# Cross attention with transposed scores, row maxima subtracted on TensorE, and division after the values

## What is computed

```python
q = _rope(_heads(xq @ wq)); k = _rope(_heads(k)); v = _heads(v)     # 16 heads of 64
sim = jnp.einsum('bhnd,bhmd->bhnm', q, k) * DH ** (-0.5)            # n = 1024, m = 77
a = jax.nn.softmax(sim, axis=-1)
o = jnp.einsum('bhnm,bhmd->bhnd', a, v)
return o.transpose(0, 2, 1, 3).reshape(B, N, MID) @ wo + bo          # + x
```

## Time and profile before

| | us |
|---|---|
| median of 3 runs (2480.9 to 2484.71) | 2481.2 |
| the profiled execution, its own time | 2478.87 |
| its span, first to last instruction | 2477.1 |
| cross attention, first to last instruction of its own | 1719.9 to 2241.8 |
| PE busy in the span | 2228.5 (90%) |
| DVE busy | 1860.5 (75%) |
| ACT busy | 1330.3 (54%) |
| POOL busy | 355.7 (14%) |

### The profile page before, as it was taken

The page is one execution under the profiler, slowest core; times in us unless marked ns, Lnnn a source line. Parts: engine busy times, 40 slices in busy tenths (PEclk is TensorE's granted clock), DMA queues, the critical chain, the costliest instruction groups (busy, mean ns, idle before and its releaser), DMA issues. The chain is left out here.

```text
span 2477.1 us, 40034 instructions
## 1 busy us (share of the span) xinstructions
PE 2228.5 (90%) x15036; PEld 1042.1 (42%) x15036; DVE 1860.5 (75%) x2924; ACT 1330.3 (54%) x1655; POOL 355.7 (14%) x201
## 2 busy tenths in 40 slices
PE   2499999999999999999999999944899999994899
PEld 2133333344333344333334333442465656563566
DVE  6579989877989886899986998574766666666453
ACT  5266666755676654666664666443443443444221
POOL 3100000000000000000000000023554545452000
PEclk9699999999999999999999999967898999986899
DMA  5101010101111011101010110052322222224211
GB/s 163 54 35 36 35 44 35 39 32 44 52 40 40 27 44 44 52 27 44 35 44 35 52 36 27 19 160 72 94 85 85 85 85 85 85 85 128 67 38 34
DMA packets 106254, 143.81 MB, mean 58 GB/s; under 512 B 28209, under 2 KB 74367, under 8 KB 106111
## 3 DMA queue, kind: packets, MB, share of 16 engines
q1 hardware_dynamic: 106111, 141.87, 17.9%
HBM read 55.70 MB, written 12.85 MB: 28 GB/s over the span
## 5 line engine op out<-in xcount | busy, mean ns | idle before, releaser
L642 PE MATMUL sa_ps_o<-sa_probs,sa_v_pair 128*64 128x512 f32 x2048 | 532.7, 614 | 2.9 <-DVE sa_mx L897 2.9
L806 ACT ACTIVATE sa_probs<-sa_ps_s 128x1024 f32<-128x1024 f32 x512 | 495.8, 1025 | 27.9 <-PE sa_ps_s L629 27.9
L897 DVE CUSTOM_DVE_ANT_0 sa_rise<-sa_ps_t,sa_rise 128x512 f32<-128x512 f32 x504 | 327.9, 688 | 190.7 <-PE sa_ps_t L606 190.3
L910 DVE TENSOR_TENSOR sa_acc<-sa_acc,sa_probs 128x1024 f32<-128x1024 f32 x384 | 462.6, 1246 | 7.2 <-ACT sa_probs L806 7.2
L794 ACT ACTIVATE sa_rise<-sa_ps_t 128x1024 f32<-128x1024 f32 x252 | 257.7, 1023 | 250.0 <-PE sa_ps_t L599 250.0
L642 PEld LDWEIGHTS sa_ps_o<-sa_probs,sa_v_pair 128*64 128x64 f32 x2048 | 101.9, 134 | 246.4 <-issue 173.7
L576 POOL TENSOR_TENSOR sa_xr<-sa_xr,sa_bo_row 128x1024 f32<-128x1024 f32 x8 | 21.6, 2726 | 1280.1 <-DMA sa_xr<-in_x 1280.1
L622 PE MATMUL sa_ps_s<-sa_hi 64*128 64x512 f16 x1024 | 194.5, 376 | 0.0
L622 PE MATMUL sa_ps_s<-sa_hi,sa_lo 64*128 64x512 f16 x1024 | 194.4, 376 | 0.0
L622 PE MATMUL sa_ps_s<-sa_lo,sa_hi 64*128 64x512 f16 x1024 | 194.4, 376 | 0.0
L629 PE MATMUL sa_ps_s<-sa_m_line,sa_m_ones 64*128 64x512 f16 x1024 | 189.5, 377 | 3.7 <-DMA sa_m_line<-sa_m_rows 3.7
(11 more groups left out here) (275 smaller groups left out, 4613.5 us busy)
## 6 DMA issues: line engine op xcount, KB each, us to landing
sa_swp<-sa_raw SPq DMA_DIRECT2D x128, 256.0 KB, 2.4
ca_swp<-ca_raw SPq DMA_DIRECT2D x70, 256.0 KB, 2.4
sa_inv<-sa_scratch SPq DMA_DIRECT2D x128, 128.0 KB, 2.9
ca_q_hl<-ca_hi SPq DMA_DIRECT2D x68, 128.0 KB, 2.3
ca_q_hl<-ca_lo SPq DMA_DIRECT2D x68, 128.0 KB, 2.3
sap_xs<-in_x SPq DMA_DIRECT2D x4, 1024.0 KB, 7.1
sa_xr<-in_x SPq DMA_DIRECT2D x4, 1024.0 KB, 5.9
cap_xs<-x_after_self SPq DMA_DIRECT2D x4, 1024.0 KB, 7.2
```

The lines of the kernel that those rows point to most:

```text
L642: ins = pe.matmul(ps_o[rows(x), half(c)], v_pair[:, kt, rows(x)], probs[:, kt % 2, c, half(x)], start=(kt == 0), stop=(kt == NK - 1))
L806: act.activation(probs[:, kt % 2, c, :], ps_s[c][:, :], ACT.Exp, scale=float(DH) ** -0.5).then_inc(s_p, 1)
L897: dve.tensor_tensor_reduce(out=larger, in0=max_banks(j, t)[:, half(x)], in1=larger, scale=1.0, scalar=-3.0e38, op0=ALU.add, op1=ALU.max, a ...
L910: dve.tensor_tensor(acc[:, c, :], before, probs[:, kt % 2, c, :], ALU.add).then_inc(s_acc[c], 1)
```

## The change

`project_context` leaves the keys where they are made, in `k_hi` and `k_lo` (128 partitions, a pair of heads each), and its stacking DMAs are gone. `cross_attention` is new. Its loops are unrolled over g = 0 to 31. For each pair, by engine, in program order:

```diff
 TensorE
+            for g in range(G):
+                bases(g)                    # queries on partitions, hi x hi only, 16 products of 77 columns
+                project(g + 3, 0)           # waits: s_sum_r (sums of g - 2 evacuated)
+                pe.transpose(turn[1][0:2 * TT, 0:P], mx[:, g % 2, :], ident[:, :]).then_inc(s_mt, 1)
+                scores(g)                   # keys on 77 partitions, 12 products of 512 columns
+                values(g - 1)
+                pe.wait_ge(s_line, 16 * (g + 1))
+                shift(g)                    # 4 products: minus the row of maxima
+                totals(g - 1)               # 4 products of ones with the probabilities
+                project(g + 3, 1)
+                if output_batch(g) is not None: ...   # g = 10, 18, 26: the 8 output tiles
 ScalarE
+                evacuate_q(g + 3, 0)
+                row(g)                      # 16 x 128, waits for the transpose
+                high_output(g - 3)
+                exponentials(g, 0); exponentials(g, 1)
+                evacuate_o(g - 1, 0); evacuate_o(g - 1, 1)   # waits: s_pv, s_ot >= g - 2
+                evacuate_sums(g - 1)
+                evacuate_q(g + 3, 1)
+                high(g + 2)
 VectorE
+                maxima(g)                   # one reduce_max over 16 x 77 elements of PSUM
+                divide(g - 3)
+                turned(g + 2)               # two multiplications with the tables, one addition
+                low_output(g - 3)
+                reciprocals(g - 2)
+                low(g + 2)                  # waits: s_hi of g + 2
+                if output_batch(g) is not None: ...   # 8 residuals
 SyncE
+                gather_sums(g - 2)
+                swap(g + 2)
+                line(g)
+                spread_inverses(g - 2)
+                if output_batch(g) is not None:
+                    sp.wait_ge(s_yr, TT * (b + 1))
+                    sp.dma_start(y_v[b], xr[:]).then_inc(s_out, 16)
+                    sp.wait_ge(s_out, 16 * (b + 1))
+                    sp.dma_start(xr[:], x_v[b + 1]).then_inc(s_x, 16)
```

```diff
+        ps_s = ps("ps_s", [P, 2, N])
+        ps_o = ps("ps_o", [P, N])
+        ps_t = ps("ps_t", [P, N])
+            def line(j):
+                sp.wait_ge(s_mt_r, j + 1)
+                sp.dma_start(m_line[0:P:DH, :], m_rows[:]).then_inc(s_line, 16)
+            def gather_sums(g):
+                sp.wait_ge(s_sum_r, g + 1)
+                sp.dma_start(few[:], sums[0:P:32, :]).then_inc(s_few, 16)
+            def spread_inverses(g):
+                sp.wait_ge(s_rec, g + 1)
+                sp.dma_start(scratch.rearrange("n (i k) -> (n i) k", k=16), few[:]).then_inc(s_scr, 16)
+                sp.wait_ge(s_scr, 16 * (g + 1))
+                for x in range(2):
+                    sp.dma_start(inv[rows(x), :], scratch[2 * x:2 * x + 2].rearrange("a k -> (a k)")
+                                 .partition_broadcast(DH)).then_inc(s_inv, 16)
+            def bases(g):
+                for t in range(TT):
+                    at = t // 4 * HALF + t % 4 * M
+                    for x in range(2):
+                        ins = pe.matmul(ps_s[:, x, at:at + M],
+                                        hi[rows(x), g % 3, t * P:(t + 1) * P], k_hi[rows(x), pair, b, :],
+                                        start=True, stop=True)
+            def scores(g):
+                for c in range(2):
+                    for n, (k, q) in enumerate(((k_hi, hi), (k_lo, hi), (k_hi, lo))):
+                        for x in range(2):
+                            pe.matmul(ps_s[0:M, c, half(x)], k[rows(x), pair, b, :], q[rows(x), s, half(c)],
+                                      start=(n == 0), stop=False)
+            def maxima(g):
+                dve.wait_ge(s_base, g + 1)
+                banks = ps_s.rearrange("p c (x n) -> p (c x) n", x=2)[:, :, 0:4 * M]
+                dve.reduce_max(mx[:, g % 2, :], banks.rearrange("p a (t m) -> p a t m", m=M), AX_X).then_inc(s_max, 1)
+            def exponentials(g, c):
+                act.wait_ge(s_st, 2 * g + c + 1)
+                act.activation(probs[:, g % 2, c, :], ps_s[0:M, c, :], ACT.Exp, ...)
```

More of the change, by code:

```diff
@@ L1043, in _ @@
             for n in range(2):
[L1044 to L1051, removed]
+                sp.wait_ge(s_swap[n], 32)
         @block.tensor
@@ L1273, in transposes @@
-            def transposes(par, x):
-                for t in range(TT):
-                    ins = pe.transpose(ps_pt[0:M, t * P:(t + 1) * P], e[:, par, x, t, :], ident[:, :])
-                ins.then_inc(s_pt_w, 1)
+                b, pair = j // PAIRS, j % PAIRS
+                cols = slice(pair * P, (pair + 1) * P)
+                split_product(pe, turn[c], range(KD), wq, xT, lambda k: (slice(None), k, cols),
+                              lambda k: (slice(None), b, k, half(c))).then_inc(s_q, 1)
@@ new lines, in shift, with values @@
+            def shift(g):
+                for c in range(2):
+                    for x in range(2):
+                        ins = pe.matmul(ps_s[0:M, c, half(x)], m_ones[rows(x), 0:M], m_line[rows(x), half(c)],
+                                        start=False, stop=True)
+                    ins.then_inc(s_st, 1)
+            def values(g):
+                b, pair = g // PAIRS, g % PAIRS
+                for c in range(2):
+                    pe.wait_ge(s_p, 2 * g + c + 1)
+                    if g >= 1:
+                        pe.wait_ge(s_oev, 2 * (g - 1) + c + 1)
+                    for x in range(2):
+                        at = pair * P + DH * x
+                        ins = pe.matmul(ps_o[rows(x), half(c)], v_all[:, b, at:at + DH], probs[:, g % 2, c, half(x)],
+                                        start=True, stop=True)
+                    ins.then_inc(s_pv, 1)
@@ L1322, in _ @@
[L1322 to L1330 removed]
+            pe.wait_ge(s_init, 3)
@@ new lines, in _ @@
+            values(G - 1)
+            pe.wait_ge(s_sum_r, G - 1)
+            totals(G - 1)
+            most = KM - 3
+            pe.wait_ge(s_ot, G - 3)
+            for t in (0, 1, 2, 3, 5, 4, 6, 7):
+                if t == 0:
+                    pe.wait_ge(s_p, 2 * G)
+                if t == 5:
+                    pe.wait_ge(s_mt_r, G)
+                if t == 4:
+                    pe.wait_ge(s_sum_r, G)
+                if t == 6:
+                    pe.wait_ge(s_oev, 2 * G)
+                output(B - 1, t, range(most), True, False)
@@ L1458, in feed_forward @@
+            for g in range(G - 3, G):
+                divide(g)
+                low_output(g)
+                if g < G - 1:
+                    reciprocals(g + 1)
+            dve.wait_ge(s_xb, 2 * B)
+            for t in range(TT):
+                residual(B - 1, t)
 def feed_forward(nc, tag, x_src, x_dst, b1, b2, xT, w1, w2):
```

490 lines of the change are left out of this document (233 added, 257 removed).

## The result

The changed kernel takes 2517.1 us (median of 4 runs, 2515.7 to 2521.7) against 2481.1 for the kernel before (2477.7 to 2484.7 in the same comparison): a ratio of 1.0148, with a 95% interval of 1.0129 to 1.0167. The forecast was 2500 with a range of 2450 to 2525: the time lies inside the range, but the change is 36 us where 19 were forecast. The profiled execution has a span of 2515.2 us, 38.1 more than before; the next stage starts at 2281.1 instead of 2241.8, which is 39.3 later, so that all of it comes from the changed stages.

A forecast was written before the change was run, and what follows sets the result against it. Bound: a closed chain from VectorE's maxima through TensorE and ScalarE back, 11.6 us, plus clock falls. First maxima 1731.8 + intervals 483.9 + tail 45 = 2260.7 against 2241.8, 19 later: 2500 by the median, range 2450 to 2525.

The forecast's parts named there:

- The closed chain: Cross attention: VectorE's maxima through transpose, scores, values, shift, exponentials, evacuations, high, low to the next maxima; 11.6 us at full clock.
- A second chain is as long, SyncE's round hides.: Cross attention: low_output releases the values' evacuation, leading back to low_output, 11.8 us less overlaps; SyncE's inverses, sums, swap about 11.2, hidden.
- A sign that the prediction had put under "wrong": VectorE's divide waiting for the inverses in cross attention would count against the forecast; no size given.
- The clock: TensorE idle 2.8 us before each transpose: one clock fall per iteration, 1.75 us taken, ends 0 and 3.5; period 13.3.
- a period of 12.4 to 12.8: In-between rival: falls in half of the iterations, or several links two tenths shorter; 2478 to 2490; chance 0.18.
- The bases: TensorE's 16 products of 64 rows: at most 0.9 us by the skill page, 2.2 without it; outside the chain.
- The iteration behind the output projection: Iterations 11, 19, 27: SyncE waits 4.4 us for the store before the maxima row; 17.4, or 20.8 if queued; 19.3 taken.
- Head: Cross attention's start to the first row maxima: swap, turned, high and two lows, 18.2 us.
- Last interval and tail: Last interval 9.5 us, without high or low; then inverse round trips, last matmuls, residual and store, 45, ends 38 and 50.
- Warm: Rival: the clock does not fall in cross attention; period 11.6, 2454; chance 0.21.
- cold: Rival: idle time and a thinner queue keep the lower clock through scores and values; period 15.1, 2547; chance 0.07.
- The order is not the bound: Rival: engine work, not program order, sets the period; TensorE 9.4, VectorE 9.0; period 9.5, about 2400; chance 0.04.

The follow-up runs named there:

- the first experiment: Changed kernel with VectorE's low(g+1) moved behind maxima(g), instead of low(g+2) at the iteration's end: 2505.0 us, ratio 1.0105 to the kernel before.
- both edits together: Changed kernel with low(g+1) behind maxima(g) and reciprocals(g-2) right behind divide(g-3) on VectorE: 2450.4 us, ratio 0.9881 to the kernel before.
- the filled gap: Changed kernel with 11 unread products in TensorE's idle time ahead of each maxima transpose, except behind an output projection: 2496.9 us, ratio 1.0070.
- the queue moved: Changed kernel with y's store, the wait for its landing and the next x's load on GpSimd's queue instead of SyncE's: 2484.7 us, ratio 1.0019.
- the narrow bias: Changed kernel with GpSimd adding the output bias to 8 columns of x only, the rest left out: 2504.8 us, ratio 1.0094.
- the order mended and the queue moved: Changed kernel with low(g+1) behind maxima(g), reciprocals(g-2) behind divide(g-3), and y's store and x's load on GpSimd's queue: 2427.5 us, ratio 0.9791.

## Why the prediction was near, and where it was off

The time lay in the range, and the mechanism of the ordinary iterations was right. The closeness is in part luck: the stage ends 39 us later than before, not 19, and the largest term, 23 ordinary intervals, came out because the forecast had halved a span of 0 to 3.5 us for the clock. Forecast and measured, by the prediction's own terms, for the profiled execution:

| term | forecast | measured | difference |
|---|---|---|---|
| start of the stage | 1713.6 | 1715.9 | +2.3 |
| from there to the first M | 18.2 | 20.4 | +2.2 |
| interval 0 | 11.9 | 9.9 | -2.0 |
| 23 ordinary intervals | 305.9 | 304.7 | -1.2 |
| 3 with an output projection | 98.7 | 97.9 | -0.8 |
| 3 behind one | 57.9 | 73.3 | +15.4 |
| last interval | 9.5 | 11.7 | +2.2 |
| tail | 45 | 47.3 | +2.3 |
| next stage starts | 2260.7 | 2281.1 | +20.4 |

- **The closed chain.** Right. The trace has full-clock intervals of 11.5 against a sum of 11.6; the first three intervals are 8.1 to 9.6 once low has left the chain; and cutting it at a second place has about the same effect. Its links: maxima 1.434 against 1.43 worked out from the earlier trace rows; values 1.94 with 1.86 until the shift, 1.87 taken from the earlier trace rows.
- **"A second chain is as long, SyncE's round hides."** The second loop is what limited the first experiment, but not the one through s_ot that the prediction had, whose way to M over the evacuations, high and low is cut by the same move: it runs through the reciprocals and the inverses' transfers, as the gain of both edits together shows. The swap lands in 3.2 us (median), not the 2.4 of the earlier trace rows, and the inverses in 3.9, so that "about 11.2" was low. It did not matter for the forecast while the first chain was longer, but a fix of the first chain alone, priced by it, was priced too high (the first experiment's expectation). A sign that the prediction had put under "wrong" was there too: the divide waits for the inverses in 8 of the 23 ordinary intervals, for 0.5 to 1.3 us. VectorE waits for high behind it in any case.
- **The clock.** One fall per iteration at 1.7 was a good mean of a wrong picture. There are 21 falls in 31 intervals, and an ordinary interval has no slow stretch (8 of 23), a short one (8, 1.4 us longer) or one of 10.2 us (7, 4.0 longer). The forecast took the middle of its ends 0 and 3.5, and the mean came out at 1.75 over 11.5: the number was right by luck. The upper end was too low, since a slow stretch of 10.2 us also covers totals and projection, and these hold back the evacuations. That the falls cost time is shown by the filled gap (-20.2 us), though the fill's own cost hides how much in all. (Among the rivals, a period of 12.4 to 12.8 at 2.6 us per 0.1 us gives 2477 to 2487, not 2478 to 2490; nothing hangs on it.)
- **The bases.** The 16 products take 0.46 us (the row at 1792.62 above), less than the 0.9 of the forecast and far from 2.2: what products of alternating shape cost in the earlier trace rows does not carry over to one shape. The Trainium skill ("TensorEngine Tiling (Array Packing)", section Key Properties) gives no time, but states that a change of the tiling mode drains the array, and the trace agrees with it. The bases lay off the chain, as said.
- **The iteration behind the output projection: the term that was mis-sized.** Forecast "17.4 or 20.8; I take 19.3", measured 24.4. The mechanism was right (the store's wait on SyncE ahead of the row: with the queue moved, 11.8). Three sizes were off in the first one: SyncE stands 5.9 us at the store, not 4.4 (4.3 and 5.0 in the other two); the longer case held, in which the row and swap queue behind the load (the row is issued at 1906.97 and released the shift at 1911.39, 4.4 us later, and each of the swap's two parts landed 5.1 to 5.2 us after its own issue), and the turned queries begin at M+13.3, not M+12.4; and turning takes 6.5 us, not 3.7, because GpSimd is adding the bias beside it. The last is 2.4 to 2.9 us of each interval by the narrow bias, and the prediction had no term for it: GpSimd's elementwise work was there counted as removed. The 11.8 with the queue moved is without this collision too, so that not all of the difference is the store's wait. The rule of the Trainium skill on ring order ("DMA: Bandwidth & Descriptors", section Queues, rings and completion order) gives the longer case, and this trace agrees with it, but does not show that ring order is the cause: with the load in GpSimd's queue SyncE's next transfer took 4.2 to 5.5 us instead of 1.4, so that one queue in common is not needed for the delay. What makes it is open.
- **Head.** The 2.2 us from stage start to first M are the same slow products (2.29 and 3.36 us instead of 1.22 each): without GpSimd's work it is 17.0, under the 18.2, so that the forecast was 1.2 too long in the rest. The start of the stage varies by itself, from 1711.0 to 1716.3 over the runs of kernels that are the same up to there, so that +2.3 says nothing.
- **Last interval and tail.** +2.2 and +2.3. The last maxima come after VectorE has waited 6.66 us for the bases. In the tail VectorE waits 5.88 and 6.15 us for the inverses of the last two pairs, where the forecast had round trips of 5.1; that is 1.8 of the 2.3. No experiment was made on either.
- **The rivals.** "Warm" (11.6) and "cold" (15.1) are both there, as kinds of interval in one execution, and the mean lies between. "The order is not the bound" (9.5, about 2400) is refuted for the changed kernel. With the order mended and the queue moved the time comes near it (2427.5), but the ordinary intervals are 11.46, not 9.5.

## What to carry to other kernels

- Lead in the number of iterations does not loosen a loop that the engines' own program orders close. Walk from the costliest reduction through each engine's queue back to itself, and do the same for the second longest loop before pricing a fix: with two of near equal length, cutting one alone gave 12 us and the other 1, cutting both 67.
- A store that SyncE waits out holds up every small transfer behind it. Look for what is queued behind the wait; moving it to an idle queue gave 32 us (some 8 of them because GpSimd's addition moved with it, by the narrow bias), moving it within the same queue 5, hardly more than the spread.
- When GpSimd's work is said to be gone, look for what is left of it and at what VectorE does in that time.

## What was not expected of the hardware

- VectorE's two-input products of 128x1024 f32 take 1.22 us alone and up to 3.37 beside GpSimd's addition of the same kind (2.8 times), one waiting out the other; with GpSimd's addition cut to 8 columns the product with the sine table never takes more than 1.22 in the same stretch.
- Nearly equal idle times of TensorE (2.46 and 2.57 us, in neighbouring iterations of the same work) brought a fall of the clock once and none the other time. Over the 23 ordinary intervals, a fall begins in 12, 1.3 to 2.9 us behind M, around the end of the idle piece (in one of them a second one begins 12.4 behind M). That piece was 2.57 us long in ten of the 12, and 1.5 to 2.46 in ten of the 11 without a fall; but one of 2.57 brought none and one of 2.19 did, and most of the shorter ones stand behind a slow interval. What decides is open.
- A small transfer in SyncE's queue is held up by a 1 MB load in GpSimd's: it takes 4.2 to 5.5 us to land instead of 1.4, in all three places. Another queue alone does not get it past the load.
- Store and load issued from GpSimd's queue take 0.9 us of it each, against 0.38 on SyncE's (1.03 for the first one), and no cost of it is to be seen here.
